# A four-layer graph network on one core: the last layer's activations transposed by VectorE in 32x32 blocks, in place of TensorE through PSUM

## The reference

```python
def _L0(h, A, W, a):     # attention
    Wh = h @ W
    e = leaky_relu(Wh @ a[:512] + swapaxes(Wh @ a[512:]), 0.2)
    return elu(softmax(where(A > 0.5, e, NEG), axis=1) @ Wh)
def _L1(h, A, W, b):     # normalised adjacency with self loops
    return relu(An @ h @ W + b)
def _L2(h, A, W):
    return relu(A @ h @ W) * row_mask
def _L3(h, A, W):        # own features beside the neighbours' mean
    agg = (A @ h) / max(deg, 1e-6)
    return relu(concat([h, agg]) @ W.T)
```

## Time and profile before

| | |
|---|---|
| median of 3 runs | 2620.7 us (2620.21 to 2622.87) |
| profiled execution, its own time | 2621.74 us |
| its span in the trace | 2619.9 us |
| PE busy | 2547.1 us, 97% |
| DVE busy | 1823.2 us, 70% |
| ACT busy | 1408.7 us, 54% |
| POOL busy | 1185.2 us, 45% |
| mean granted TensorE clock | 0.992 of full speed |

### The profile page before, as it was taken

One profiled execution on the slowest core, in us unless ns is written; L12 is line 12 of the kernel. 1 busy time (PEld: TensorE's weight loads), 2 busy tenths in 40 slices (PEclk: granted clock), 3 DMA queues, 4 the chain that ended last, 5 costly groups with the idle time before them and its releaser, 6 DMA issues.

```text
span 2619.9 us, 40393 instructions
## 1 busy us (share of the span) xinstructions
PE 2547.1 (97%) x13704; PEld 2205.5 (84%) x13704; DVE 1823.2 (70%) x4251; ACT 1408.7 (54%) x2571; POOL 1185.2 (45%) x1607
## 2 busy tenths in 40 slices
PE   2799999999999999999999999999999999999998
PEld 2688888888888888888888888888888888888886
DVE  6776676676676677677677777777776766766753
ACT  3555555555555555555555555555555555555542
POOL 2544444444444444444444444444444444444431
PEclk8899999999999999999999999999999999999999
DMA  4101111111011011011111111111111111111000
GB/s 140 41 29 49 33 41 49 33 41 49 30 44 49 29 45 49 29 45 46 33 45 41 37 45 41 37 45 35 42 46 33 41 49 33 41 49 33 29 17 25
DMA packets 72844, 109.30 MB, mean 42 GB/s; under 512 B 4288, under 2 KB 37056, under 8 KB 72640
## 3 DMA queue, kind: packets, MB, share of 16 engines
q1 hardware_dynamic: 72640, 106.71, 12.6%
HBM read 73.14 MB, written 33.55 MB: 41 GB/s over the span
## 4 chain that ended last, share of the span: by engine, by line
PE 96%; DVE 1%; issue 1%; ACT 1%; POOL 1%; DMA 0%; SPq 0%; POOLq 0%; ACTq 0%; DVEq 0%
PE O L277 46%; PE T L277 34%; PE X L277 13%; PE X L310 2%; PE X L298 1%; POOL h_lo L747 0%; ACT h L405 0%; DMA act_out<-w_all 0%; POOL xs L712 0%; DVE p_lo L589 0%; DVE scores L522 0%; DVE w_lo L512 0%; DVE t_lo L595 0%; ACT act_out L436 0%; DVE xs L630 0%
## 5 line engine op out<-in xcount | busy, mean ns | idle before, releaser
L747 POOL TENSOR_TENSOR h_lo<-h,h_hi 128x512 fp32r<-128x512 f32 x384 | 503.4, 1333 | 673.1 <-ACT h_hi L411 673.1
L595 DVE TENSOR_TENSOR t_lo<-T,t_hi 128x512 fp32r<-128x512 f32 x512 | 352.5, 690 | 399.1 <-ACT t_hi L417 399.1
L405 ACT ACTIVATE h<-xs,ln_bias,ln_scale 128x512 f32<-128x512 f32 x512 | 396.0, 811 | 391.9 <-POOL ln_bias L741 391.9
L277 PE MATMUL O<-w_hi,t_hi 128*128 128x512 f32 x1536 | 603.2, 393 | 0.0
L277 PE MATMUL O<-w_hi,t_lo 128*128 128x512 f32 x1536 | 598.2, 389 | 0.0
L277 PE MATMUL O<-w_lo,t_hi 128*128 128x512 f32 x1536 | 598.1, 389 | 0.0
L417 ACT CAST t_hi<-T 128x512 fp32r<-128x512 f32 x512 | 298.3, 584 | 257.1 <-PE T L277 257.1
L712 POOL TENSOR_TENSOR xs<-xs,act_out 128x512 f32<-128x512 f32 x128 | 163.7, 1297 | 531.7 <-ACT act_out L439 496.9
L277 PEld LDWEIGHTS O<-w_hi,t_lo 128*128 128x128 f32 x1536 | 288.3, 188 | 60.2
L277 PEld LDWEIGHTS O<-w_hi,t_hi 128*128 128x128 f32 x1536 | 288.5, 188 | 55.9 <-DVE t_lo L595 0.5
L277 PEld LDWEIGHTS O<-w_lo,t_hi 128*128 128x128 f32 x1536 | 288.6, 188 | 55.7
(11 more groups left out here) (92 smaller groups left out, 4991.4 us busy)
## 6 DMA issues: line engine op xcount, KB each, us to landing
xs<-x SPq DMA_DIRECT2D x64, 512.0 KB, 3.6
out<-xs SPq DMA_DIRECT2D x64, 512.0 KB, 2.8
a_raw<-adj_t SPq DMA_DIRECT2D x64, 256.0 KB, 2.7
a_rows<-adj SPq DMA_DIRECT2D x64, 256.0 KB, 2.7
xs<-w_all SPq DMA_DIRECT2D x6, 512.0 KB, 7.3
act_out<-w_all SPq DMA_DIRECT2D x2, 512.0 KB, 6.7
z<-w_all SPq DMA_DIRECT2D x2, 512.0 KB, 6.4
v_rows<-a_vecs SPq DMA_DIRECT2D x1, 512.0 KB, 5.4
```

The costliest lines, as they stand in the source:

```text
L277: last = nc.tensor.matmul(psum, s, m, start=(start and n == 0 and i == 0), stop=(stop and n == len(pairs) - 1 and i == 2))
L405: nc.scalar.activation(h[:, k.odd, m], xs[:, k.xb, m], ACT.Relu, bias=ln_bias[:, k.quad, m:m + 1], scale=ln_scale[:, k.quad, m:m + 1], acc ...
L595: nc.vector.tensor_tensor(t_lo[:, k.odd, c], T[:, c], t_hi[:, k.odd, c].bitcast(F32), ALU.subtract).then_inc(t_lo_ready, 1)
L747: nc.gpsimd.tensor_tensor(h_lo[:, k.odd, m], h[:, k.odd, m], h_hi[:, k.odd, m].bitcast(F32), ALU.subtract).then_inc(h_lo_ready, 1)
```

## The change

`transpose_h` is gone from PE, with its eight transposes per graph, and so are the waits that kept PSUM X free for it. DVE gets `turn`: sixteen `transpose` instructions per graph, one for each pair of a source quadrant i (nodes) and a target quadrant o (features). Each takes 32 partitions by 256 elements (eight 32x32 blocks: 2 node tiles by 4 feature tiles) from h and writes 32 partitions by 256 elements into `act_out[:, 1]`, which serves as buffer for hT (128x1024). Eight of them stand at the end of slot k-3 after `dots`, eight in slot k-2 after `add_mask`. ACT then writes ht_hi in one instruction of 128x1024 from SBUF, and DVE ht_lo in one of 128x1024 from two SBUF operands; before it was two of 128x512 each, from PSUM.

```diff
-            def transpose_h(k):
-                wait(pe, h_ready, k.done(ALL, NT))
...
-                for half in range(2):
-                    for f in range(HALF * half, HALF * half + HALF):
-                        for m in range(NT):
-                            c = (f % HALF) * N + m * P
-                            last = nc.tensor.transpose(X[:, half, c:c + P], h[:, k.odd, m, f * P:f * P + P], ident[:])
-                    last.then_inc(ht_psum_ready, 1)
...
             def project_first(k):
...
-                wait(pe, ht_lo_ready, k.done(L3, NT))
+                wait(pe, ht_lo_ready, k.done(L3))
...
-                if step(j + 2).layer == 3:
-                    transpose_h(step(j + 2))
...
             def transposed(k):
                 wait(act, z_psum_ready, k.done(L3, NT, back=4))
...
+                wait(act, ht_ready, k.done(L3, TURNS))
+                nc.scalar.copy(flat(ht_hi[:]), ht).then_inc(ht_hi_ready, 1)
...
+        ht = flat(act_out[:, 1])
+        ht_blocks = ht.rearrange("p (c m q n) -> p m c q n", c=FT, m=NT, q=QUADS)
+        h_blocks = h[:].rearrange("p b m (c q f) -> p b m c q f", c=FT, q=QUADS)
...
+            def turn(k, blocks):
+
+                wait(dve, h_ready, k.done(ALL, NT))
+                wait(dve, l1_done, k.done(L1, back=3))
+                for n in blocks:
+                    i, o = divmod(n, QUADS)
+                    nc.vector.transpose(ht_blocks[QUAD * o:QUAD * o + QUAD, :, :, i],
+                                        h_blocks[QUAD * i:QUAD * i + QUAD, k.odd, :, :, o]).then_inc(ht_ready, 1)
...
             def transposed(k):
...
+                wait(dve, ht_hi_ready, k.done(L3))
+                nc.vector.tensor_tensor(flat(ht_lo[:]), ht, flat(ht_hi[:]).bitcast(F32),
+                                        ALU.subtract).then_inc(ht_lo_ready, 1)
...
             def scaled_relu(k):
...
+                wait(dve, ht_lo_ready, k.done(L3, back=-2))
...
                 if step(j + 3).layer == 0:
                     add_mask(step(j + 3))
+                if step(j + 3).layer == 3:
+                    turn(step(j + 3), range(TURNS // 2))
                 if step(j + 2).layer == 3:
+                    turn(step(j + 2), range(TURNS // 2, TURNS))
                     transposed(step(j + 2))
```

More of the change, by code:

```diff
@@ L12 @@
 P = 128
+QUAD = 32
+QUADS = P // QUAD
+TURNS = QUADS * QUADS
 LAYERS = 4
@@ L85, in sem, with flat @@
             return ctx.enter_context(nc.semaphore(name))
+        def flat(t):
+            return t.rearrange("p m n -> p (m n)")
         w_hi = sb("w_hi", [P, WEIGHTS, FT, F], F32R)
@@ L161, in gnn_kernel @@
         t_ready, o_ready = sem("t_ready"), sem("o_ready")
-        wh_rows_ready, ht_psum_ready, z_psum_ready = sem("wh_rows_ready"), sem("ht_psum_ready"), sem("z_psum_ready")
+        wh_rows_ready, ht_ready, z_psum_ready = sem("wh_rows_ready"), sem("ht_ready"), sem("z_psum_ready")
         stats_ready, mv_ready, neg_mean_ready, var_ready, rstd_ready, scale_ready, ln_ready = (
@@ L196, in tiles @@
             return dram[g].rearrange("(m p) f -> p m f", p=P)
-        def flat(t):
-            return t.rearrange("p m n -> p (m n)")
         def flat_blocks(t):
@@ L293, in spread @@
                 wait(pe, wh_ready, k.done(L0, DOTS))
-                wait(pe, ht_lo_ready, k.done(L3, NT, back=1))
                 wait(pe, scores_ready, k.done(L0, NT, back=4))
@@ L300, in spread @@
                 last.then_inc(wh_rows_ready, 1)
-            def transpose_h(k):
-                wait(pe, h_ready, k.done(ALL, NT))
-                wait(pe, z_ready, k.done(L3, NT, back=4))
-                wait(pe, scores_ready, k.done(L0, NT, back=3))
-                for half in range(2):
-                    for f in range(HALF * half, HALF * half + HALF):
-                        for m in range(NT):
-                            c = (f % HALF) * N + m * P
-                            last = nc.tensor.transpose(X[:, half, c:c + P], h[:, k.odd, m, f * P:f * P + P], ident[:])
-                    last.then_inc(ht_psum_ready, 1)
             def gather(k):
@@ L401, in activate @@
                 wait(act, wh_ready, k.done(L0, DOTS, back=2))
-                wait(act, ht_psum_ready, k.done(L3, NT, back=2))
+                wait(act, ht_ready, k.done(L3, TURNS, back=2))
                 for m in range(NT):
@@ L596, in gathered @@
                                         ALU.subtract).then_inc(t_lo_ready, 1)
-            def transposed(k):
[L599 to L603, removed]
+            def turn(k, blocks):
[5 more added lines that the diff above has]
+                                        h_blocks[QUAD * i:QUAD * i + QUAD, k.odd, :, :, o]).then_inc(ht_ready, 1)
+            def transposed(k):
+                wait(dve, ht_hi_ready, k.done(L3))
+                nc.vector.tensor_tensor(flat(ht_lo[:]), ht, flat(ht_hi[:]).bitcast(F32),
+                                        ALU.subtract).then_inc(ht_lo_ready, 1)
             def positive_part(k):
```

## The result

The changed kernel takes 3043.1 us (median of 4 runs, 3042.75 to 3044.14) against 2620.7 us: 1.161 times as long, 95% interval 1.159 to 1.162. The forecast was 2931 us in a range of 2750 to 3060. The direction and the mechanism came out as predicted; the size, 422 us against 310, is a third larger.

A forecast was written before the change was run, and what follows sets the result against it. PE, busy 97% of the span, was taken as the bound. A 3.63 us later `project_first` plus 1.54 us of low clock, 5.17 us per period for 60 graphs, add 310 us: 2931 us, range 2750 to 3060.

The forecast's parts named there:

- The saving on PE: On PE, dropping eight transposes per graph frees 0.87 us per period, 56 us in all if nothing else moved.
- The anchor: The start of `dots` on DVE, tied to PE's gather of step k-2, was claimed to stay.
- the chain of DVE from the end of `dots` to `project_first`: DVE's work in line, with sixteen turns added, was claimed to start `project_first` 3.63 us later per period.
- the collision: On DVE, `add_mask` beside POOL's late additions was claimed to take 1.21 us instead of 0.42.
- The price of a turn: Distance D between turn starts on DVE, taken as 0.42 us, the whole duration of a 256-element instruction.
- The rival of overlapping turns: On DVE, turns start 0.34 us apart, giving 2855 us; chance 0.20.
- The fall of the clock: On PE in `project_first`, behind 4.5 us idle, matmuls at 1.2 GHz were claimed to cost 1.54 us every period.
- What else is late: Statistics, softmax and p_lo behind ht_lo come later, but were claimed to cost nothing.
- the cover of 1.6 us: Room between the second t_lo, 9.3 us after `project_first` starts, and PE's next gather, 10.95 us after.
- The ends of the run: The last four graphs, costed at nothing since PE waits for ht_lo there already (1.72, 2.50 us).
- a D of 0.55: Upper end of the range: turns on DVE 0.55 us apart, 7.25 us per period, 3060 us.
- The rival on the other side: PE doesn't wait: sixteen turns fit in 2.2 us of slack, D 0.14 us, 2565 us; chance of faster 0.04.

The follow-up runs named there:

- experiment 2: Changed kernel with two turns per graph instead of sixteen, the rest of hT not written: 2578.1 us, 0.984 of the kernel before.
- experiment 1: Changed kernel with all sixteen turns of a graph reading and writing quadrant 0: 2844.8 us.
- experiment 3: Changed kernel with 20 matmuls on constant operands put on PE before `project_first`'s wait: 2923.1 us.
- experiment 7: Changed kernel with `project` of layer 2 before `project_first` on PE, so hT is needed 5.4 us later: 2851.7 us.
- experiment 5: Changed kernel with eight turns per graph instead of sixteen, half of hT not written: 2684.5 us.
- experiment 8: Experiment 7 with ACT's and DVE's orders also fitted to the turns: 2637.4 us; the kernel before with these orders as far as they fit: 2636.7 us.
- experiment 9: Experiment 8's changed kernel with `add_mask` and a_diag of `with_self` moved from DVE to POOL: 2620.05 us, 0.9997 of the kernel before.
- experiment 10: Experiment 9 with a_diag waiting for DVE's last `mean_relu` operation: 2616.5 us; also with the last three graphs transposed on PE: 2603.7 us.

## Why the prediction was right, and where its sizes were off

**The saving on PE**, 0.87 us per period: right, 0.91 in experiment 2, and swallowed whole by the wait, as forecast.

**The anchor, and the chain of DVE from the end of `dots` to `project_first`**: right in every link, and `add_mask` had the 1.21 us of the collision (in the kernel before, four of its 64 were slow, not one). The chain was forecast 3.63 us longer and is 4.44.

**The price of a turn** is the link that was mis-sized: 0.465 us instead of 0.42, 16 x 0.045 = 0.72 of the missing 0.81 us. Another 0.10 is `add_mask`, which takes 1.23 us of DVE, not 1.13: the first turn behind it doesn't overlap it. I had taken the whole duration of an ordinary 256-element instruction. A turn lasts 0.436 (0.39 in experiment 1), and in the changed kernel each starts another 0.03 us behind the end of the one before. The duration as the price was the right idea; 0.015 us of duration and 0.03 us behind it were missing, and no row cited for the price could show either. The rival of overlapping turns is out: only on one quadrant, in experiment 1, do they overlap.

**The fall of the clock**: forecast in each period at 1.54 us, measured 2.03 (experiment 3). The direction came from rows 7; the size came from a single one of these cases. It is right for every second period, 45.57 - 39.57 - 4.44 = 1.56 us; in the others the stretch at 1.2 GHz is longer, and the price is 2.6. And whether the clock falls at all isn't a matter of the idle time alone: at 3.0 and 3.1 us it fell in 34 and in 36 periods of 59 (experiments 1 and 7), at 1.4 us never (experiment 5), and yet once behind 2.50 us. Every idle time of 5.1 us brought it.

**What else is late**: the cover of 1.6 us behind `project_first` held; PE waits nowhere else in the steady period. The count of matmuls of one gather in the text ahead of the prediction is wrong (24, not 48); the 10.95 us used there is that of two products.

**The ends of the run**: the second mis-sized term. I costed the last four graphs at nothing since PE waited there already. They cost 28.6 us: the sixteen turns are in line between `activate` and ht_hi whether DVE has other work or not, and with less work on PE they are less covered, not more. PE's longest wait, 11.9 us, is the last graph's. The start cost 7.4 us more, which I hadn't counted either.

Sum of the misses: 59 x 0.81 = 48, 59 x (2.08 - 1.54) = 32, ends 36, against one full period (5 us) counted more; 111 of the 112 us. That 3043 lies within the range owes something to luck: its room above 2931 was given to a D of 0.55, while D alone brought less than half of the miss; clock and ends, the rest of it, had been given none.

**The rival on the other side** (all sixteen turns within the slack) didn't come, at 0.465 against a break-even of 0.19. But it needed neither faster turns nor the slack that the kernel had: experiments 7 to 10 made the slack, by moving the reader of hT instead of its writer.

## What to carry to other kernels

Before work goes from the engine that is the bound to one that is idle 30% of the time, look where that idle time lies: if it isn't between the new work and its reader, the time goes into the bound engine's wait, and that wait may take the clock with it. A moved load wants moved deadlines: the same sixteen instructions cost 16% in the old order and gained 0.7% once their result was needed 5.4 us later, DVE's other work was fitted around them and two small steps of it went to POOL, and the last graphs, where nothing covers them, kept the old way. Cost the pipeline's filling and emptying for themselves. And before an order is called free, look at the starts: a wait shorter than a record is long shows in no account of idle time.

## What was not expected of the hardware

- VectorE instructions on 32 partitions that move from quadrant to quadrant start 0.465 us apart, on one quadrant 0.33 us; the instruction itself lasts 0.436 or 0.39 us.
- Behind the same idle time of 5.1 us in each period matmuls run at half the clock for 3.2 us in one and for 5.3 us in the next, in strict alternation; at 3.0 us of idle time it falls in 34 periods of 59.
- A VectorE instruction with one source, `add_mask`, that starts beside one of POOL's additions takes 1.21 us instead of 0.42, always until 0.28 us or so after the end of that addition.
- `add_mask` on POOL takes 1.95 us (experiment 9), on DVE 0.42.
